# Two heads side by side in the rows of TensorE's array, in 48 rows each, for the narrow attentions' scores

## Chip, core and metric

One NeuronCore of one Trainium2 chip runs the whole program; the other cores are idle. The metric is the device time of the program in microseconds. The engines are named as in the profile: PE is TensorE's matmul, PEld its weight load, DVE VectorE, ACT ScalarE, POOL GpSimd, SP SyncE, which issues the DMAs.

## What is computed

The reference is two layers over x of shape (2, 1024, 128): a wide attention (16 heads of 64, 4 key heads, rope, low-rank additions), an expert stage with a Sinkhorn gate, a normalized narrow attention, the expert stage again, a windowed narrow attention, then a block (narrow attention and a second kind of expert stage), an RWKV scan and the same block again. The change touches the four narrow attentions, which have 16 heads of 8 channels. The block's is

```python
att = jnp.einsum('bhqd,bhkd->bhqk', q, k) / jnp.sqrt(jnp.asarray(hd, x.dtype))
att = jnp.where(causal, att, jnp.asarray(-jnp.inf, att.dtype))
att = jax.nn.softmax(att, axis=-1)
y = jnp.einsum('bhqk,bhkd->bhqd', att, v)
```

The one called "normalized" here (L0_attn_b) divides q and k by their norms first, so its scores are small and the kernel leaves out the row maximum. The windowed one (L1_attn_a) cuts queries into windows of 128 and masks each with a triangle that begins at key 0, so only the first 128 keys count.

## The kernel before

**Parts.** q and k are float32. `four_heads` splits each into three bfloat16 parts (L658 to L672 on ACT, L715 to L719 on DVE, and for the second batch entry L704 on POOL), stores them to DRAM (L511) and loads them as stacks (L491, L493): 72 partitions hold all nine products of a part of q and a part of k for the 8 channels. A score is then one bfloat16 matmul with a contraction of 72. Where the maximum is used, three further rows (72 to 74) hold the shift, split into three parts, on the q side and ones on the k side.

**Units and groups.** Four heads are a group; there are 8 groups in an attention, 4 for each batch entry. A unit is one block of 128 keys against 512 queries. A causal attention has 12 units to a group, numbered here u0 to u11: u0 to u3 (queries 0 to 511, with 512, 384, 256 and 128 of them still in play) and u4 to u11 (queries 512 to 1023, with 512 in play in u4 to u8, then 384, 256, 128). Eight of them, u0 to u3 and u8 to u11, meet the diagonal. The windowed one has 2 units to a group.

**The order on PE** is written out by hand (L629 to L644). Step u of a group does: `cols` for heads 0 and 1 (scores by key, L545; where the unit meets the diagonal and the maximum is used, a mask is added by a matmul of 128 rows, L550), some row jobs, `values` of two earlier units in every second step (L567, float32, four heads in the four 32-column tiles of the array, drained into bank 7), `cols` for heads 2 and 3, and the rest of the row jobs. ACT takes the exponentials of two heads at a time (L685); DVE and ACT move the finished sums (L656, L654), and PE turns them (L626, "divide").

**Row jobs** exist where the maximum is used: scores by query (L579) for the *next* group, one bank of PSUM each, with a mask where they meet the diagonal (L583); DVE reduces each bank to its maximum (L758). A causal group has 38: 2 "quads", 4 "pairs", 8 "three", 20 "full" (4 of them masked) and 4 "tail"; they are spread over steps 0 to 8. Steps 9 to 11 have none. They go round a ring of three banks: PE waits on `job_read` until job n-3 has been read before it writes job n (L614 to L616). After the last one DVE splits the maxima (L724 to L732), PE turns them (L621, "turn", in step 9), DVE copies them (L767), SP issues four DMAs into rows 72 to 74 of the q stack (L501), and `cols` of u0 of the next group waits for them (L539).

Of the kernel before, what the change touches and what calls it, by code (L numbers as in the profile page):

```python
# [388 lines left out]
PBUFS, LAG = 4, 2  # L389


def row_jobs(nk):
# [3 lines left out]
    return ([("quads", (a, a + 1), 0) for a in (0, 2)] + [("pairs", (i,), 1) for i in range(4)]  # L396
# [4 lines left out]
def side_jobs(ng, nu, nk, use_max, lead):  # L401
# [34 lines left out]
def four_heads(S, Q, K, V, AO, nk, tri, use_max, SLOTS):  # L436

    units, PS, nu, ng = units_of(nk), S.PS, len(units_of(nk)), B * NH // 4  # L440
# [8 lines left out]
    rows_of_stack = 75 if use_max else 72  # L449
# [3 lines left out]
    chunks = [(split_b(x)[:, b, :], dst, b) for b in range(B)  # L453
              for x, dst in ((Q, S.q_parts), (K, S.k_parts.rearrange("b d j h t -> b j d h t")))]
# [13 lines left out]
    with phase(S, 27) as (block, sems):  # L468
# [10 lines left out]
        def slot(g, i):  # L479
            return 4 * (g % SLOTS) + i  # L480

        @block.sync
        def _(sp):
            def load_group(g):
                b, h0 = divmod(4 * g, NH)
                if g >= SLOTS:
                    sp.wait_ge(cols_ready, 2 * nu * (g - SLOTS + 1))
                sp.wait_ge(stored[b], 16 * 6)
                at = slice(slot(g, 0), slot(g, 0) + 4)
                for copy in range(3):  # L490
                    sp.dma_start(S.Kst[24 * copy:24 * (copy + 1), at, :],  # L491
                                 S.k_parts[b, :, :, h0:h0 + 4, 0:keys].rearrange("d j h t -> (d j) h t")).then_inc(loaded[g % SLOTS], 16)
                    sp.dma_start(S.Qst[copy:72:3, at, :],  # L493
                                 S.q_parts[b, :, :, h0:h0 + 4, :].rearrange("j d h t -> (j d) h t")).then_inc(loaded[g % SLOTS], 16)

            def load_c(e):
# [3 lines left out]
                for i in range(4):  # L500
                    sp.dma_start(S.Qst[72:75, slot(g, i), HALF * sides[0]:HALF * (sides[-1] + 1)],  # L501
                                 S.ct[w * i:w * (i + 1), k % 2, :]).then_inc(c_loaded[g % SLOTS], 16)

            if use_max:
                for row in range(72, 75):
                    sp.dma_start(S.Kst[row:row + 1, :, :], S.ones_b[0:4 * SLOTS * keys // P, :]).then_inc(ones_set, 16)
            def store_batch(b):
                for i in range(3):
                    for n in (2 * b, 2 * b + 1):
                        sp.wait_ge(part_done, 2 * i + n % 2 + 6 * b + 1)  # L510
                        sp.dma_start(chunks[n][1][b, i].rearrange("d h t -> h d t"), S.parts[:, n % 2, i, :]).then_inc(stored[b], 16)  # L511

            store_batch(0)
            for g in range(max(lead, 1)):
                load_group(g)
            for e in turns:
# [15 lines left out]
        def _(pe):  # L532
            def cols(U, i):
# [1336 lines left out]
```

## Time and profile before

| | us |
|---|---|
| median of three runs | 2785.84 |
| lowest, highest | 2783.70, 2789.19 |
| profiled execution, own time | 2787.93 |
| its span, first to last instruction | 2786.2 |

The narrow attentions take the stretches 1150 to 1346 (normalized), 1536 to 1672 (windowed), 1701 to 2030 and 2306 to 2633 us (the two blocks') of the span. A page lists busy time by engine, then the costliest groups of instructions by source line: busy time and mean duration, and the idle time in front of them with what ended it. In a timeline each row gives start, length, engine, line, operation, shapes (partitions x elements; for a matmul contraction*columns of the array), and how many instructions of the kind follow one another; the bracket is the engine's idle time before and what ended it. PEclk and the ninth column of a stretch's row are TensorE's granted clock as a share of 2.4 GHz.

### The profile page before, as it was taken

To read this page: it belongs to the slowest core of one execution; us is meant where nothing else is said; L and a number is where in the kernel's file an instruction comes from. 1 tells how busy PE (TensorE), PEld (TensorE's weight loads), DVE (VectorE), ACT (ScalarE), POOL (GpSimd) and SP (SyncE) were. 2 spreads that over 40 slices of the span, in tenths; PEclk is the share of its full clock that TensorE was granted. 3 is DMA by queue.
4 is the path that set the end of the run, shared out by engine and by line. 5 is a ranking of instruction groups with operands and counts; after the bars stand their busy time and mean duration, and the time that the engine had idled before them with its cause. 6 is when DMAs were issued, how large, how long until landed. Compare 5 with 4: busy or idle time off the path is not lost. (4 is left out here: it accounts for less than half of the span.)

```text
span 2786.2 us, 37366 instructions
## 1 busy us (share of the span) xinstructions
PE 2224.0 (80%) x13838; PEld 1285.9 (46%) x13838; DVE 1588.6 (57%) x3402; ACT 1437.1 (52%) x2136; POOL 804.1 (29%) x384
## 2 busy tenths in 40 slices
PE   4999999999999718499619485999979425999888
PEld 2656666666666415333315243344347212444357
DVE  4777777776776445411355444777433685777324
ACT  2666676666766351388542243455642312555541
POOL 2677777776776201322001203100000022000000
PEclk8899999999999858699759696899989656999999
DMA  2000000000000130321310312211010002210000
GB/s 71 8 1 1 3 8 1 3 8 1 1 3 1 53 103 1 81 67 35 100 56 1 93 33 56 61 36 36 2 31 1 1 0 70 64 36 19 1 31 16
DMA packets 41660, 82.91 MB, mean 30 GB/s; under 512 B 10744, under 2 KB 18472, under 8 KB 37320
## 3 DMA queue, kind: packets, MB, share of 16 engines
q1 hardware_dynamic: 41480, 80.52, 10.7%
q8 instruction: 112, 1.84, 0.3%
q14 instruction: 68, 0.56, 0.1%
HBM read 66.11 MB, written 13.63 MB: 29 GB/s over the span
## 5 line engine op out<-in xcount | busy, mean ns | idle before, releaser
L685 ACT ACTIVATE probs<-psum_banks 128x1024 f32<-128x1024 f32 (+3 forms) x608 | 474.3, 826 | 367.2 <-PE psum_banks L550 260.0
L1096 POOL TENSOR_SCALAR l0a_rows<-l0a_rows,l0a_rinv 128x1024 f32<-128x1024 f32 x192 | 562.2, 2935 | 253.5 <-DVE l0a_rinv L1074 253.3
L758 DVE TENSOR_REDUCE neg_max<-psum_banks 128x1 f32<-128x512 f32 (+3 forms) x672 | 398.8, 658 | 201.4 <-PE psum_banks L583 149.7
L1062 DVE TENSOR_REDUCE l0a_nmax<-psum_banks 128x1 f32<-128x1024 f32 x256 | 312.9, 1222 | 208.7 <-PE psum_banks L955 208.0
L545 PE MATMUL psum_banks<-q_stack,k_stack 75*128 75x512 bf16 (+7 forms) x1216 | 324.9, 345 | 74.5 <-ACT probs L685 25.6
L1009 ACT ACTIVATE l0a_rows<-psum_banks,l0a_nmax 128x1024 f32<-128x1024 f32 x256 | 285.9, 1117 | 81.8 <-DVE l0a_nmax L1062 79.3
L579 PE MATMUL psum_banks<-k_stack,q_stack 72*128 72x128 bf16 (+3 forms) x1024 | 250.3, 328 | 78.1 <-DMA q_stack<-q_parts 66.5
L969 PE MATMUL psum_banks<-packed,l0a_rows 128*128 128x128 f32 x2048 | 267.7, 274 | 7.8 <-POOL l0a_rows L1096 6.3
L954 PE MATMUL psum_banks<-l0a_kh,l0a_qw 128*128 128x512 f32 x512 | 257.4, 503 | 6.1 <-DVE l0a_qw L1030 5.8
L969 PEld LDWEIGHTS psum_banks<-packed,l0a_rows 128*128 128x128 f32 x2048 | 237.9, 141 | 52.5 <-POOL l0a_rows L1096 11.5
L567 PE MATMUL psum_banks<-probs,v_ones 128*32 128x512 f32 (+3 forms) x2432 | 245.8, 520 | 7.5 <-ACT o_sum L654 6.5
L545 PEld LDWEIGHTS psum_banks<-q_stack,k_stack 75*128 75x128 bf16 (+1 forms) x1216 | 106.5, 101 | 254.6 <-ACT probs L685 104.5
L955 PE MATMUL psum_banks<-l0a_kl,l0a_qw 128*128 128x512 f32 x512 | 205.8, 402 | 0.0
L579 PEld LDWEIGHTS psum_banks<-k_stack,q_stack 72*128 72x128 bf16 x1024 | 95.3, 105 | 201.8 <-DVE neg_max L758 90.3
L954 PEld LDWEIGHTS psum_banks<-l0a_kh,l0a_qw 128*128 128x128 f32 x512 | 97.8, 191 | 134.6 <-issue 79.0
L1004 ACT ACTIVATE x_norm<-psum_banks 128x512 f32<-128x512 f32 x128 | 75.9, 593 | 136.8 <-PE psum_banks L969 136.7
L1677 POOL TENSOR_TENSOR rw_b<-rw_k,rw_o 128x1024 f32<-128x1024 f32 x2 | 4.0, 1998 | 459.2 <-DVE rw_o L1692 459.2
L550 PE MATMUL psum_banks<-tri_k,ident_b 128*128 128x128 bf16 (+1 forms) x576 | 133.8, 249 | 0.0
L1623 DVE SCALAR_TENSOR_TENSOR l1f_y<-psum_banks,rt_g,l1f_y 128x128 f32<-128x128 f32 x256 | 72.1, 344 | 103.5 <-PE psum_banks L1561 103.5
L1585 ACT ACTIVATE l1f_h<-psum_banks 128x512 f32<-128x512 f32 x128 | 75.7, 599 | 105.5 <-PE psum_banks L1547 105.2
L981 PE MATMUL psum_banks<-x_norm,l0a_v 128*64 128x512 f32 x512 | 124.0, 604 | 3.7 <-ACT l0a_ot L1014 3.7
L1547 PE MATMUL psum_banks<-x_norm_t,l1f_w 128*128 128x512 f32 x256 | 115.7, 610 | 12.4 <-DMA l1f_w<-in_l1f_w 10.8
(270 smaller groups left out, 3420.9 us busy)
## 6 DMA issues: line engine op xcount, KB each, us to landing
q_stack<-q_parts SPq DMA_DIRECT2D x96, 192.0 KB
k_stack<-k_parts SPq DMA_DIRECT2D x72, 192.0 KB
qkv<-in_l0f_w SPq DMA_DIRECT2D x6, 1024.0 KB, 5.3
q_parts<-parts SPq DMA_DIRECT2D x24, 256.0 KB
k_parts<-parts SPq DMA_DIRECT2D x24, 256.0 KB
moe_b<-in_l0f_b SPq DMA_DIRECT2D x32, 128.0 KB, 4.7
l1f_w<-in_l1f_w SPq DMA_DIRECT2D x16, 256.0 KB, 4.9
moe_w<-in_l0f_w SPq DMA_DIRECT2D x2, 1024.0 KB, 5.5
```

The costliest lines, as they stand in the source:

```text
L545: m = pe.matmul(PS[:, bank, c0:HALF], S.Kst[0:rows_of_stack, slot(g, i), kt * P:(kt + 1) * P], S.Qst[0:rows_of_stack, slot(g, i), side * H ...
L550: m = pe.matmul(PS[:, bank, c0:c1], S.ident_b[:], S.tri_k[:, 0:c1 - c0], start=False, stop=True, skip_group_check=True)
L567: m = pe.matmul(PS[32 * i:32 * (i + 1), 7, c0:HALF], S.Vx[:, NT * b + kt, h0 + i, :], S.Pt[:, U % PBUFS, i, c0:HALF], start=kt == 0, stop= ...
L579: return pe.matmul(bank[:, at:at + k1 - k0], S.Qst[0:72, slot(g, i), jq * P:(jq + 1) * P], S.Kst[0:72, slot(g, i), k0:k1], start=first, st ...
L685: act.activation(S.Pt[:, U % PBUFS, 2 * half:2 * half + 2, c0:HALF], PS[:, bank:bank + 2, c0:HALF], ACT.Exp).then_inc(exp_done, 1)
L758: dve.tensor_reduce(out, scores, AX, ALU.max, negate=True).then_inc(job_read, 1)
L954: pe.matmul(scores(s)[:, c0:c0 + HALF], q, R.Kh[:, b, c0:c0 + HALF], start=True, stop=False)
L955: m = pe.matmul(scores(s)[:, c0:c0 + HALF], q, R.Kl[:, b, c0:c0 + HALF], start=False, stop=True)
L969: m = pe.transpose(PS[:, 4 + a, jj * P:(jj + 1) * P], R.Pr[:, (NT * ps + 2 * jj + a) % RING, kt * P:(kt + 1) * P], S.ident[:])
L1009: act.activation(R.Pr[:, s % RING, :], scores(s), ACT.Exp, bias=R.nmax4[:, s % 4:s % 4 + 1], accum_out=R.rsum4[:, s % 4:s % 4 + 1]).then_i ...
L1062: dve.tensor_reduce(R.nmax4[:, s % 4:s % 4 + 1], scores(s), AX, ALU.max, negate=True).then_inc(max_done, 1)
L1096: pool.tensor_scalar(R.Pr[:, s % RING, :], R.Pr[:, s % RING, :], R.rinv4[:, s % 4:s % 4 + 1], None, ALU.mult).then_inc(pool_normed, 1)
```

## The change

The three smallest of the nine products are left out: parts (i, j) of q and k are multiplied only where i + j is at most 2, which makes six products of 8 channels, 48 rows (51 with the shift). Heads 0 and 2 of a group lie in partitions 0 to 50, heads 1 and 3 in 64 to 114. The two matmuls of a `cols` call follow one another, one in each half of the array's rows, and the two masks come behind both. Row jobs are issued two at a time, the matmuls of the two alternating, then their masks; the wait on `job_read` is that of the second of the two, taken ahead of both. The spread of jobs over steps is in twos (6 in step 0, 4 in steps 1 to 8; before 5, 4, 4, 4, 5, 4, 4, 4, 4). k's parts are stored six times instead of three (9 stores to a batch entry instead of 6), the stacks are loaded by 8 DMAs of 2/3 of the bytes instead of 6, and the ones (L506) are written by 6 DMAs behind the first loads instead of 3 ahead of the stores. Sizes of tiles in SBUF halve.

```diff
-PBUFS, LAG = 4, 2
+PBUFS, LAG, PRODUCTS = 4, 2, 6 * HD8
...
-    return ([("quads", (a, a + 1), 0) for a in (0, 2)] + [("pairs", (i,), 1) for i in range(4)]
+    return ([("quads", (a, a + 2), 0) for a in (0, 1)] + [("pairs", (i,), 1) for i in range(4)]
...
-        for k, e in enumerate(events):
-            steps[s0 + k * n // len(events)].append(e)
+        for k in range(0, len(events), 2):
+            steps[s0 + k * n // len(events)] += events[k:k + 2]
...
-    rows_of_stack = 75 if use_max else 72
+    rows_of_stack = PRODUCTS + 3 if use_max else PRODUCTS
...
+    key_blocks = ((0, 1, 2), (3, 4), (5,))
...
-            return 4 * (g % SLOTS) + i
+            return 2 * (g % SLOTS) + i // 2
+
+        def half(i, r0, r1):
+
+            return slice(64 * (i % 2) + r0, 64 * (i % 2) + r1)
...
-                sp.wait_ge(stored[b], 16 * 6)
-                at = slice(slot(g, 0), slot(g, 0) + 4)
-                for copy in range(3):
-                    sp.dma_start(S.Kst[24 * copy:24 * (copy + 1), at, :],
-                                 S.k_parts[b, :, :, h0:h0 + 4, 0:keys].rearrange("d j h t -> (d j) h t")).then_inc(loaded[g % SLOTS], 16)
-                    sp.dma_start(S.Qst[copy:72:3, at, :],
-                                 S.q_parts[b, :, :, h0:h0 + 4, :].rearrange("j d h t -> (j d) h t")).then_inc(loaded[g % SLOTS], 16)
+                sp.wait_ge(stored[b], 16 * 9)
+                at = slice(slot(g, 0), slot(g, 0) + 2)
+                for i in range(2):
+                    heads = slice(h0 + i, h0 + i + 3, 2)
+                    sp.dma_start(S.Kst[half(i, 0, PRODUCTS), at, :],
+                                 S.k_parts[b, :, :, heads, 0:keys].rearrange("c d h t -> (c d) h t")).then_inc(loaded[g % SLOTS], 16)
+                    for r0, parts in ((0, 3), (24, 2), (40, 1)):
+                        sp.dma_start(S.Qst[half(i, r0, r0 + HD8 * parts), at, :],
+                                     S.q_parts[b, 0:parts, :, heads, :].rearrange("j d h t -> (j d) h t")).then_inc(loaded[g % SLOTS], 16)
...
-            def cols(U, i):
-                (g, u), n = divmod(U, nu), (4 * U + i) // 2
+            def cols(U, h):
+                (g, u), n = divmod(U, nu), 2 * U + h
...
+                masks = use_max and meets(units[u])
+                for i in (2 * h, 2 * h + 1):
+                    rows = half(i, 0, rows_of_stack)
+                    m = pe.matmul(PS[:, 2 * (n % pairs) + i % 2, c0:HALF], S.Kst[rows, slot(g, i), kt * P:(kt + 1) * P],
+                                  S.Qst[rows, slot(g, i), side * HALF + c0:(side + 1) * HALF], start=True, stop=not masks,
+                                  skip_group_check=True)
+                c1 = HALF if tri == "window" else c0 + P
+                for i in range(2 if masks else 0):
+                    m = pe.matmul(PS[:, 2 * (n % pairs) + i, c0:c1], S.ident_b[:], S.tri_k[:, 0:c1 - c0], start=False,
                                   stop=True, skip_group_check=True)
...
+            def scores(two):
+
+                n, g = number[two[-1]], two[0][1]
+                if n >= len(ring):
+                    pe.wait_ge(job_read, n - len(ring) + 1)
...
+                for k in range(len(pieces(two[0]))):
+                    last = []
+                    for e in two:
+                        i, jq, c0, k0, k1 = pieces(e)[k]
+                        rows = half(i, 0, PRODUCTS)
+                        last.append(pe.matmul(spare(e, HALF)[:, c0:c0 + k1 - k0], S.Qst[rows, slot(g, i), jq * P:(jq + 1) * P],
+                                              S.Kst[rows, slot(g, i), k0:k1], start=k == 0, stop=False, skip_group_check=True))
+                for e, m in zip(two, last):
+                    if e[2][0] != "full" or e[2][2] == 3:
+                        m = cover(e)
+                    m.then_inc(job_ready, 1)
...
-                mid = sum(e[0] == "rows" for e in events) // 2 if U >= 0 else 0
+                mid = sum(e[0] == "rows" for e in events) // 4 * 2 if U >= 0 else 0
...
-        S.Qst, S.Kst = S.sb("q_stack", [P, 4 * SLOTS, T], BF16), S.sb("k_stack", [P, 4 * SLOTS, P * nk(NT - 1)], BF16)
+        S.Qst, S.Kst = S.sb("q_stack", [P, 2 * SLOTS, T], BF16), S.sb("k_stack", [P, 2 * SLOTS, P * nk(NT - 1)], BF16)
```

`pieces(e)` lists the matmuls of a row job as `scores` made them before, and `cover(e)` is its mask.

## Rows read from the trace of the kernel before

**Rows 1.** The page: busy time, and the costliest groups of the narrow attentions.

```profile
PE 2224.0 (80%) x13838; PEld 1285.9 (46%) x13838; DVE 1588.6 (57%) x3402; ACT 1437.1 (52%) x2136; POOL 804.1 (29%) x384
...
L758 DVE TENSOR_REDUCE neg_max<-psum_banks 128x1 f32<-128x512 f32 (+3 forms) x672 | 398.8, 658 | 201.4 <-PE psum_banks L583 149.7
...
L545 PE MATMUL psum_banks<-q_stack,k_stack 75*128 75x512 bf16 (+7 forms) x1216 | 324.9, 345 | 74.5 <-ACT probs L685 25.6
```

**Rows 2.** Stretches: one steady group of the block's attention. Columns as named.

```profile
core 0: us, PE busy (x) PEld busy (x) DVE busy (x) ACT busy (x) POOL busy (x), PEclk, DMA share, GB/s
...
1856.00:1890.00 34.00, 31.73 (x258) 14.64 (x255) 24.46 (x50) 19.98 (x27) 0.00 (x0) 1.00 0.16 36
```

**Rows 3.** Timeline of PE, same group: first matmul of u0, u5, u9, and around values.

```profile
1860.45 0.38 PE L545 MATMUL psum_banks<-q_stack,k_stack 75*128 75x512 bf16 x1 [0.93 <-issue]
...
1871.86 0.59 PE L579 MATMUL psum_banks<-k_stack,q_stack 72*128 72x512 bf16 x2
1872.29 0.59 PE L545 MATMUL psum_banks<-q_stack,k_stack 75*128 75x512 bf16 x2
...
1874.22 0.39 PE L579 MATMUL psum_banks<-k_stack,q_stack 72*128 72x512 bf16 x1 [0.15 <-DVE neg_max L758]
...
1881.19 0.66 PE L579 MATMUL psum_banks<-k_stack,q_stack 72*128 72x512 bf16 x2
1881.78 1.92 PE L567 MATMUL psum_banks<-probs,v_ones 128*32 128x512 f32 x16
1883.64 0.60 PE L545 MATMUL psum_banks<-q_stack,k_stack 75*128 75x512 bf16 x2
...
1886.73 0.33 PE L545 MATMUL psum_banks<-q_stack,k_stack 75*128 75x384 bf16 x1
```

**Rows 4.** Timeline of DVE and SP, same group.

```profile
1861.64 4.28 DVE L758 TENSOR_REDUCE neg_max<-psum_banks 128x4 f32<-128x512 f32 x7 [5.51 <-PE psum_banks L583]
...
1872.27 5.21 DVE L758 TENSOR_REDUCE neg_max<-psum_banks 128x1 f32<-128x512 f32 x9 [0.99 <-PE psum_banks L579]
...
1884.50 3.68 DVE L758 TENSOR_REDUCE neg_max<-psum_banks 128x1 f32<-128x512 f32 x6 [1.41 <-PE psum_banks L579]
...
1890.15 3.00 SPq L501 DMA_DIRECT2D q_stack<-c_turned  x4
```

**Rows 5.** Timeline of PE, wide attention: matmuls of 8 rows between ones of 128.

```profile
824.82 0.71 PE L924 MATMUL psum_banks<-l0a_ob,l0a_oa 8*128 8x128 f32 x4
825.46 0.50 PE L954 MATMUL psum_banks<-l0a_kh,l0a_qw 128*128 128x512 f32 x1
825.79 0.39 PE L955 MATMUL psum_banks<-l0a_kl,l0a_qw 128*128 128x512 f32 x1
826.02 0.40 PE L954 MATMUL psum_banks<-l0a_kh,l0a_qw 128*128 128x512 f32 x1
```

**Rows 6.** Timeline of PE, windowed attention: four row jobs between two cols calls.

```profile
1618.42 0.39 PE L579 MATMUL psum_banks<-k_stack,q_stack 72*128 72x128 bf16 x4
1618.65 0.38 PE L583 MATMUL psum_banks<-tri_q,ident_b 128*128 128x512 bf16 x1
...
1620.27 0.38 PE L545 MATMUL psum_banks<-q_stack,k_stack 75*128 75x512 bf16 x1
```

**Rows 7.** Timeline of ACT, normalized attention, from 1261.5 us; and its stretch.

```profile
1268.04 7.01 ACT L685 ACTIVATE probs<-psum_banks 128x256 f32<-128x256 f32 x8 [0.98 <-PE psum_banks L545]
1275.39 3.56 ACT L685 ACTIVATE probs<-psum_banks 128x1024 f32<-128x1024 f32 x4 [0.34 <-PE psum_banks L545]
...
1240.00:1260.00 20.00, 18.55 (x153) 6.75 (x145) 2.48 (x6) 17.14 (x24) 4.70 (x9) 1.00 0.25 60
```

**Rows 8.** Stretches: last group of the first block's attention, which has no row jobs.

```profile
1995.00:1998.00 3.00, 1.75 (x16) 0.83 (x12) 0.00 (x0) 1.25 (x2) 0.00 (x0) 1.00 0.02 3
1998.00:2001.00 3.00, 2.78 (x22) 1.20 (x23) 0.00 (x0) 2.13 (x4) 0.00 (x0) 0.53 0.00 0
...
2007.00:2010.00 3.00, 2.43 (x16) 0.67 (x8) 0.00 (x0) 1.41 (x3) 0.00 (x0) 0.76 0.00 0
```

**Rows 9.** Start of the first block's attention: last store, first load, first row job.

```profile
1708.36 0.52 SPq L511 DMA_DIRECT2D k_parts<-parts  x1
...
1711.25 0.33 SPq L491 DMA_DIRECT2D k_stack<-k_parts  x1
...
1720.51 0.61 PE L579 MATMUL psum_banks<-k_stack,q_stack 72*128 72x128 bf16 x4 [20.57 <-DMA q_stack<-q_parts]
```

More of the change, by code:

```diff
@@ L515, in _ @@
                 load_group(g)
+            for i in range(2 if use_max else 0):
+                for row in range(PRODUCTS, PRODUCTS + 3):
+                    sp.dma_start(S.Kst[half(i, row, row + 1), :, :], S.ones_b[0:2 * SLOTS * keys // P, :]).then_inc(ones_set, 16)
             for e in turns:
@@ L539, in cols @@
                     pe.wait_ge(c_loaded[g % SLOTS], c_landed(next(e for e in turns if e[1] == g and side in e[2])))
                     if U == 0:
[L541 to L542 removed]
+                        pe.wait_ge(ones_set, 96)
+                if n >= pairs:
                     pe.wait_ge(exp_done, n - pairs + 1)
[L544 to L547 removed]
@@ L611, in scores @@
-                return m
+                    return [(i, j, 0, 0, HALF)]
+                if kind == "tail":
+                    return [(i, j, 0, HALF, T)]
+                if kind == "three":
+                    return [(i, j, 0, (j - 2) * P, (j + 1) * P)]
+                if kind == "pairs":
+                    return [(i, 1, 0, 0, 2 * P), (i, 5, 2 * P, HALF, HALF + 2 * P)]
+                if kind == "quads":
+                    return [(h, 4 * a, P * (2 * n + a), HALF * a, HALF * a + P) for n, h in enumerate(heads) for a in range(2)]
@@ new lines, in pieces, with cover @@
+                return [(i, 4 * j + n, P * n, 0, P) for n in range(4)]
+            def cover(e):
+                bank, (kind, _, j) = spare(e, HALF), e[2]
+                if kind in ("tail", "three") or kind == "full" and j == 3:
+                    c0 = 2 * P if kind == "three" else 3 * P
+                    out = bank[:, c0:c0 + P].unsqueeze(1)
+                elif kind == "pairs":
+                    out = bank.rearrange("p (n c) -> p n c", n=2)[:, :, P:]
+                else:
+                    out = bank.rearrange("p (n c) -> p n c", n=4)
+                return pe.matmul(out, S.ident_b[:], S.tri_q[:].unsqueeze(1).to_broadcast([P, out.shape[1], P]), start=False,
+                                 stop=True, skip_group_check=True)
@@ L613, in side_job, with side_jobs_of @@
+            def side_jobs_of(events):
+                rows = [e for e in events if e[0] == "rows"]
+                for k in range(0, len(rows), 2):
+                    scores(rows[k:k + 2])
+                for e in events:
+                    if e[0] != "rows":
+                        side_job(e)
             def side_job(e):
```

92 lines of the change are left out of this document (23 added, 69 removed).

## Prediction

> **What bounds the kernel now.** I read the page first, then the four stretches of the narrow attentions, then one steady group instruction by instruction. The page says PE is the busiest engine and that L545, one of the two lines halved here, has 325 us [rows 1]; from that alone one would expect a large gain. The stretch of one group says less: PE 31.7, DVE 24.5 and ACT 20.0 us busy of 34.0 [rows 2]. But a matmul's length is not what it holds PE for: two of 512 columns (0.59) are followed 0.43 later by the next, so one holds PE 0.215 us, and N columns N/2400 us [rows 3]. Counted that way a group has on PE: cols 7.7 (4 heads x 4608 columns), row jobs 7.7, their masks 1.7 each, values 7.7 plus 1.5 of gaps around them, turns 0.9, together 28.9 of 34.0 us.
>
> The rest is waits. DVE reduces 38 banks a group at one per 0.60 us (5.21 for nine) [rows 4], with the two divides (0.54 each) 23.5 us, and it has to do them within steps 0 to 8. Then comes a chain that hardly uses PE: split, turn, copy, four DMA issues, landing. DVE's reduces end at 1888.2, the DMAs are issued until 1893.15, `cols` of the next u0 starts at 1894.44 (34.0 after 1860.45, the rows of SP stand 34.0 apart too), and DVE is idle 5.51 us per group for it [rows 3, 4]. So a group is 26.3 us of steps 0 to 8 (1860.45 to 1886.73) [rows 3] and 7.7 of steps 9 to 11, of which the last 4.8 are that chain. For steps 0 to 8, take for each step the longer of PE's sum and DVE's: 3.0, 2.7, 2.9, 3.1, 3.0, 2.6, 2.9, 3.7, 2.4 = 26.3. The agreement tells me that now one engine's slack in a step is made good by the ring of three banks, and that DVE sets about half of the steps. If PE cost nothing DVE would still take 23.5, so no more than 2.8 us of 34 can be had.
>
> **The change, part by part.** *Fewer rows, two heads at once.* A contraction of 51 rather than 75 saves nothing by itself. Two matmuls in the two halves of the rows: no row of this trace has such a pair. Bounds: 0.43 for two of 512 (one after the other) and 0.215 (wholly beside each other). The nearest row is values: 16 matmuls of 512 columns, four column tiles, in 1.86 including the gaps, a quarter of what they would take in turn [rows 3]. I take 0.215 + 0.03. That removes 0.185 from each full-width pair: at most 24 cols calls and 19 pairs of jobs, 7.7 - 1.3 = 6.4 us of PE per group. The Trainium skill (TensorE: Matmul & The Clock Gate, Part 3) measured four row tiles at 3.07 times the speed of one; by that share the pair would take about 0.28 instead of 0.245, an estimate that adds 0.035 x 43 = 1.5 us of PE per group; no run here shows it yet.
>
> *Changes of the array's shape.* Masks stay matmuls of 128 rows. Where now everything but values has one shape, each masked cols call becomes half rows, full rows, half rows, and so does each masked pair of jobs: 16 + 11 calls, 54 changes a group. The price of one: into values 0.16 (1881.19 + 0.43 to 1881.78) and, at the five other values of the group, 0.10; out of them 0.15 (1881.78 + 1.71 to 1883.64) [rows 3]. For tiles of rows, four matmuls of 8 rows take 0.64 where their columns need 0.43, and the first full one behind them holds PE 0.33 instead of its twin's 0.23 [rows 5]. Bounds 0 (half and full rows might not exclude each other) to 0.16; I take 0.13, nearest the values row since it is bfloat16 on one side. 54 x 0.13 = 7.0 us: more than the 6.4 saved. PE's sum per group is no smaller after the change. The Trainium skill (TensorEngine Tiling, Key Properties) says that changing the tiling mode, not just the tile, drains TensorE. It makes no exception for rows against full; it speaks against the lower bound.
>
> *Jobs in twos over a ring of three.* The second of a pair may not be written until the job three before it, the first of the pair before, has been read. So while PE makes a pair, DVE has one bank in hand, 0.60 us, where it now has two. The loop: matmul start to reduce start 0.41 (1871.86 to 1872.27), reduce 0.68, read to next matmul 0.07 (1872.27 + 2 x 0.60 + 0.68 = 1874.15 to 1874.22) [rows 3, 4]: 1.16 to 1.2 without mask, level with DVE's 1.20 a pair; with a mask 0.245 + 0.13 + 0.25 + 0.75 = 1.38 to 1.43, with quads 1.6. And slack no longer carries over, so I take the longest of PE, DVE and loop for each *half* step (a pair of jobs with the cols call, and values, behind it). Example u7: pair 0.245, values 1.71 + 0.25, cols 0.245 = 2.45, then DVE 1.20: 3.65. u1: pair 0.19 + 0.13 + 0.11 + 0.13, values 0.64 + 0.12, cols 0.19 + 0.37 = 1.87, then 1.32: 3.19. All: 4.47, 3.19, 3.11, 3.63, 2.40, 2.88, 2.94, 3.65, 2.75 = 29.0, against 26.3. PE's own sum in these steps is 22.3 and DVE's 23.9: what costs is that each waits for the other. With changes at 0 it is 27.2. Steps 9 to 11 keep their 4.8 us chain; the turn comes 0.1 to 0.2 later, as two masked calls stand before it. Per steady group +2.8; there are six and a half per block stage, +18. The first group's 14 jobs, at half clock, lose some 0.4 per pair to the loop, +3; the last group, without jobs, gains 0.18 on eight calls and loses 0.08 on sixteen: 0. Two block stages: **+42**.
>
> *Windowed attention.* PE is nearly dense. Four jobs now take 1.85 (1618.42 to 1620.27) [rows 6]. After: the second pair starts 0.3 + 0.13 + 0.42 + 0.75 = 1.6 behind the first and takes 0.3 + 0.13 + 0.44 + 0.13: 2.6. Twice a group, six groups, +9. A cols call goes from 0.88 to 0.245 + 0.26 + 0.44 = 0.95, 32 calls: +2. The first sixteen jobs: +3. Together **+14**.
>
> *Normalized attention.* No masks, no jobs; ACT is 17.1 of 20 us busy. Cols get shorter by 0.185, which only shortens ACT's two gaps of 0.34 per group; the two of 0.98 lie behind values and stay, and one has a divide in front that now costs two changes more (+0.2) [rows 7]. -0.4 x 8, and -1 for the start at half clock: **-4**.
>
> *DMA.* Nine stores instead of six (some 0.75 MB more before the first load), ones moved out of the way (-0.8 of issue), loads of 768 instead of 1152 KB into the first group (now 9.3 from 1711.25 to 1720.51, with stores ending 2.4 after their last issue) [rows 9]. -3 for the load, +2 to +3 for the stores: 0, bounds -3 to +3 in each of four stages. Later loads are under cover of a group each. The new wait (16 * 9) holds ACT for the second batch's parts only as long as the stores take; behind it are exponentials. The split parts' arithmetic does not change.
>
> **Sum.** 42 + 14 - 4 + 0 = +52 on the profiled execution's 2787.9, which lies 2 above the median: 2838 against a median of 2786, 1.9% slower.
>
> **The rivals.** *Clock falls.* In the last group, with no row jobs, PE was 1.75 of 3 us busy at full clock and then the granted clock was 0.53, 0.5 until it rose in the stretch from 2007, so near 10 us at 1.2 GHz [rows 8]; the second block's last group looks alike. In steady groups before, it held at 1.00 [rows 2]. After, PE streams columns for about 20 of 37 us instead of 27 of 34. If the clock falls once a group, some 10 us at half rate add to u0 to u3, where the PE-bound halves grow by about 4 us: 13 groups, +52, and up to +20 in the normalized one: 2890 to 2910. For it: rows 8. Against it: I cannot tell whether two halves at once count as more activity. The skill's clock page (TensorE: Matmul & The Clock Gate, Part 1) has the clock fall after idleness; here it fell with PE over half busy.
> *Faster: no drain, ring deep enough.* If a change of shape between half and full rows costs 0, and slack still carries over a step, the step maxima give 24.7 instead of 26.3: -1.6 - 0.3 for 13 groups = -25, the windowed stage -8 (cols 0.64 instead of 0.88), the normalized -8: 2745 to 2765. It decides below some 0.05 per change. Halfway, at 0 but with the pair's loop, the time is within 5 of now.
> *Pairs don't overlap.* Then every call also loses 0.185 and PE leads everywhere: above 2900.
>
> **How the numbers follow.** Forecast as worked out (2810 to 2865): 0.44. Clock: 0.24. No overlap: 0.05. Faster: 0.20. Within 0.2%, about what a measurement of this kernel can tell from none: 0.07. The range leaves out the upper part of the second and third and the lower part of the fourth: 2762 to 2905. Faster 0.20, same 0.07, slower 0.73.
>
> **What would show it.** Right: a steady group of 36 to 38 us; PE gaps of 0.10 to 0.15 at L545 to L550 and back; DVE's reduces in twos with 0.15 to 0.25 idle between masked pairs. Wrong: matmuls of 51 rows followed by a mask after N/2400 with no gap; a group under 34 us; PE rows of half height that start 0.2 apart; granted clock under 1.00 in steady groups.

## The result, and the profile after

The changed kernel takes 2852.56 us (median, 2845.5 to 2860.1), the kernel before 2787.52 beside it: 1.0236 times as long, 95% interval 1.0202 to 1.0269. The forecast was 2838. The time came near it and on the forecast side, but not for the reasons forecast: every stage term was mis-sized (two stages cost more than forecast, two less), and the largest part of the loss was one of the rivals, the clock.

The profiled execution has a span of 2843.8 us against 2786.2; it is the fastest of the four of the kernel after, so traces differ by 57.6 us where medians differ by 65.0. A stage is counted from the first split on ACT (L669 before, L689 after) to the end of its last exponential or eviction:

| stage | before | after | difference | forecast |
|---|---|---|---|---|
| normalized attention | 193.2 | 180.1 | -13.1 | -4 |
| windowed attention | 134.5 | 135.7 | +1.2 | +14 |
| first block's attention | 326.2 | 358.8 | +32.6 | +21 |
| second block's attention | 325.7 | 357.8 | +32.1 | +21 |
| all between and behind | 1806.6 | 1811.4 | +4.8 | 0 |

Of the last row 4.2 us lie between the two blocks, from the end of the first one's attention to the first split of the second. No kernel here changes anything in that stretch, and it took between 278.2 and 285.8 us in the twelve traces (278.5 before, 282.7 after), so I don't count it for the change.

From the page of the kernel after (it answers [rows 1]): the line of `cols`, one of the two that were halved, did shrink (L556 has 211 us, L545 had 325), but DVE's reduces (L778) now wait 256 us instead of 201, longest for the masks of the row jobs (L608).

```profile
PE 2193.6 (77%) x13828; PEld 1188.5 (42%) x13838; DVE 1604.8 (56%) x3402; ACT 1435.6 (50%) x2136; POOL 803.3 (28%) x384
...
L778 DVE TENSOR_REDUCE neg_max<-psum_banks 128x1 f32<-128x512 f32 (+3 forms) x672 | 412.6, 660 | 256.3 <-PE psum_banks L608 185.7
...
L556 PE MATMUL psum_banks<-q_stack,k_stack 51*128 51x512 bf16 (+7 forms) x1216 | 211.0, 358 | 84.6 <-ACT probs L705 39.7
```

Two steady groups of the kernel after, each from one issue of the c DMAs (L509) to the next. The columns are those of [rows 2]; PEclk is the granted clock.

```profile
1900.37:1940.40 40.03, 34.54 (x257) 11.47 (x255) 25.38 (x49) 19.99 (x27) 0.00 (x0) 0.83 0.11 21
2542.17:2577.72 35.55, 29.31 (x257) 10.46 (x255) 25.36 (x49) 19.89 (x27) 0.00 (x0) 1.00 0.11 24
```

The same instructions take 35.55 us at 1.00 and 40.03 at 0.83. Of the ten groups that the kernel before ran in 34.0 us each at 1.00, the kernel after has one at 1.00; the others read 0.83 to 0.95, and the mean of the ten is 38.4. So a group has two losses: 1.55 us at full clock, and 2.9 us because TensorE drops to the lower of its two levels (1.2 GHz) inside the group, once or twice. Where it drops, in three-us stretches of the group that begins at 1862.47:

```profile
1865.00:1868.00 3.00, 2.20 (x26) 0.79 (x18) 0.00 (x0) 0.96 (x2) 0.00 (x0) 1.00 0.36 89
1868.00:1871.00 3.00, 2.29 (x19) 0.76 (x18) 2.78 (x5) 1.47 (x2) 0.00 (x0) 1.00 0.85 157
1871.00:1874.00 3.00, 2.81 (x27) 1.05 (x26) 2.11 (x4) 1.13 (x2) 0.00 (x0) 0.65 0.11 20
...
1883.00:1886.00 3.00, 1.82 (x18) 0.70 (x20) 3.00 (x7) 2.07 (x3) 0.00 (x0) 0.93 0.00 0
1886.00:1889.00 3.00, 2.99 (x24) 0.72 (x16) 1.44 (x3) 2.03 (x3) 0.00 (x0) 0.50 0.00 0
```

The first drop follows the thin stretch around the chain (split, turn, copy, DMAs), the second the steps in which PE waits for DVE (1.82 of 3 us busy). Not every group has both: of the ten, five drop 9 to 10 us behind the issue of the c DMAs (and all five again later), four only at 20 us or later, and one not at all, though all run the same instructions. What decides between them no run shows. While the clock is low PE is busy throughout (2.99 of 3.00), since the same columns take twice as long.

Now the timeline of PE in the group that ran at full clock, to read the prices of the prediction:

```profile
2546.42 0.39 PE L556 MATMUL psum_banks<-q_stack,k_stack 51*128 51x512 bf16 x2 [0.80 <-issue]
2546.74 0.29 PE L561 MATMUL psum_banks<-tri_k,ident_b 128*128 128x128 bf16 x2
2546.96 0.40 PE L624 MATMUL psum_banks<-k_stack,q_stack 48*128 48x128 bf16 x8
...
2548.47 0.39 PE L624 MATMUL psum_banks<-k_stack,q_stack 48*128 48x256 bf16 x4
2548.79 0.39 PE L608 MATMUL psum_banks<-tri_q,ident_b 128*128 128x256 bf16 x2
2549.86 0.39 PE L624 MATMUL psum_banks<-k_stack,q_stack 48*128 48x256 bf16 x4 [0.68 <-DVE neg_max L778]
...
2560.96 0.39 PE L624 MATMUL psum_banks<-k_stack,q_stack 48*128 48x512 bf16 x2 [0.56 <-DVE neg_max L778]
2561.19 0.38 PE L556 MATMUL psum_banks<-q_stack,k_stack 51*128 51x512 bf16 x2
2562.15 0.39 PE L624 MATMUL psum_banks<-k_stack,q_stack 48*128 48x512 bf16 x2 [0.59 <-DVE neg_max L778]
...
2574.41 0.34 PE L556 MATMUL psum_banks<-q_stack,k_stack 51*128 51x384 bf16 x2
```

- Two heads side by side: 2560.96 to 2561.19, 0.23 us for two matmuls of 512 columns, where the kernel before needed 0.43 [rows 3].
- Half rows to full rows: 2546.42 to 2546.74 is 0.32, of which the pair is 0.21 (its columns) to 0.23 (as measured above): 0.09 to 0.11. Back: 2546.74 to 2546.96 is 0.22, of which two masks of 128 columns are 0.107: 0.11.
- The loop of pairs: 2560.96 to 2562.15, 1.19 without mask; 2548.47 to 2549.86, 1.39 with one; 2546.96 to 2548.47, 1.51 for quads. In each PE idles until DVE has read a bank.
- u0 to u9, 2546.42 to 2574.41: 28.0 us, against 26.3 in [rows 3].

### The profile page after: what moved, and what is told of

Read it like the earlier page. It is cut to its first block and busy times, and to the rows that moved or that the text cites. A ratio compares the mean times of both kernels' runs of the same rounds, so it can differ in the third digit from the quotient of the medians.

```text
span 2843.8 us, 37453 instructions
## 1 busy us (share of the span) xinstructions
PE 2193.6 (77%) x13828; PEld 1188.5 (42%) x13838; DVE 1604.8 (56%) x3402; ACT 1435.6 (50%) x2136; POOL 803.3 (28%) x384
## 5 line engine op out<-in xcount | busy, mean ns | idle before, releaser
L778 DVE TENSOR_REDUCE neg_max<-psum_banks 128x1 f32<-128x512 f32 (+3 forms) x672 | 412.6, 660 | 256.3 <-PE psum_banks L608 185.7
L577 PE MATMUL psum_banks<-probs,v_ones 128*32 128x512 f32 (+3 forms) x2432 | 272.1, 568 | 7.6 <-ACT o_sum L674 6.5
L556 PE MATMUL psum_banks<-q_stack,k_stack 51*128 51x512 bf16 (+7 forms) x1216 | 211.0, 358 | 84.6 <-ACT probs L705 39.7
L624 PE MATMUL psum_banks<-k_stack,q_stack 48*128 48x128 bf16 (+3 forms) x1024 | 150.8, 352 | 155.9 <-DVE neg_max L778 92.1
L556 PEld LDWEIGHTS psum_banks<-q_stack,k_stack 51*128 51x128 bf16 (+1 forms) x1216 | 56.8, 95 | 260.8 <-ACT probs L705 119.7
L624 PEld LDWEIGHTS psum_banks<-k_stack,q_stack 48*128 48x128 bf16 x1024 | 41.9, 99 | 257.3 <-DVE neg_max L778 185.5
L1001 PE MATMUL psum_banks<-l0a_cols,l0a_v 128*64 128x512 f32 x512 | 124.1, 605 | 0.0
```

Source lines behind the costliest of these rows:

```text
L556: m = pe.matmul(PS[:, 2 * (n % pairs) + i % 2, c0:HALF], S.Kst[rows, slot(g, i), kt * P:(kt + 1) * P], S.Qst[rows, slot(g, i), side * HALF ...
L577: m = pe.matmul(PS[32 * i:32 * (i + 1), 7, c0:HALF], S.Vx[:, NT * b + kt, h0 + i, :], S.Pt[:, U % PBUFS, i, c0:HALF], start=kt == 0, stop= ...
L624: last.append(pe.matmul(spare(e, HALF)[:, c0:c0 + k1 - k0], S.Qst[rows, slot(g, i), jq * P:(jq + 1) * P], S.Kst[rows, slot(g, i), k0:k1], ...
L778: dve.tensor_reduce(out, scores, AX, ALU.max, negate=True).then_inc(job_read, 1)
L1001: m = pe.matmul(PS[HD * a:HD * (a + 1), 6, :], R.V[:, v // STEPS % B, kt, :], (R.Pc, R.Pd)[v // 2 % 2][:, v % 2, a, :], start=kt == 0, sto ...
```

## The experiments

Theory A: the loop of pairs and the changes of shape make the block stages slower. The rival: the clock makes them slower, because PE now streams less. The other numbers below are of steady groups, ten in each run (the mean of the kernel after is 38.4 us; two of the expectations quoted below have it as 38.6):

| kernel | ratio to before | group at clock 1.00 | mean of ten | granted clock in them |
|---|---|---|---|---|
| before | 1 | 34.0 | 34.0 | 1.00 |
| after | 1.0236 | 35.55 | 38.4 | 0.83 to 1.00 |
| masks in half rows | 1.0163 (1.0133 to 1.0193) | 34.5 | 36.4 | 0.79 to 1.00 |
| single waits | 1.0356 (1.031 to 1.0402) | none | 43.0 | 0.73 to 0.95 |
| both | 1.0024 (1.0011 to 1.0037) | 33.9 | 34.8 | 0.91 to 1.00 |
| extra matmuls, one stretch | 1.0291 (1.0266 to 1.0316) | 36.9 | 39.2 | 0.84 to 1.00 |
| single waits, extra matmuls in one stretch | one run, 2873.82 | 37.2 | 40.4 | 0.80 to 1.00 |
| extra matmuls, both stretches | 1.0157 (1.0136 to 1.0178) | 37.3 | 37.3 | 1.00 |
| before without masks | one run, 2818.65 | 33.1 | 36.4 | 0.82 to 1.00 |
| all heads in one half | one run, 3102.35 | none | 51.8 | 0.65 to 0.70 |
| both, all heads in one half | one run, 3120.49 | none | 46.35 | 0.70 to 0.84 |
| normalized attention alone | 0.9938 (0.9917 to 0.9959) | 34.0 | 34.0 | 1.00 |

**Masks in half rows** (e1_halfmasks). A second copy of identity and masks has its row halves swapped, so that each head's mask is made in its own half:

```diff
-                for i in range(2 if masks else 0):
-                    m = pe.matmul(PS[:, 2 * (n % pairs) + i, c0:c1], S.ident_b[:], S.tri_k[:, 0:c1 - c0], start=False,
-                                  stop=True, skip_group_check=True)
+                for part in range(2 if masks else 0):
+                    for i in range(2):
+                        rows = half(i, 0, 64)
+                        m = pe.matmul(PS[:, 2 * (n % pairs) + i, c0:c1], (S.ident_b, S.ident_s)[part][rows, :],
+                                      (S.tri_k, S.tri_ks)[part][rows, 0:c1 - c0], start=False,
+                                      stop=part == 1, skip_group_check=True)
```

> The changed kernel, but the causal and window masks are no longer matmuls of 128 rows: each is two matmuls of 64 rows, in the half of the array's rows in which its head's scores were made (with a second copy of the identity and of the masks whose row halves are swapped), and the masks of two heads lie side by side as the scores do. So the columns cost the same and the 54 changes between half and full rows of a steady group are gone. Theory A (shape changes, 0.11 us each, and the loop of job pairs over three banks made the block stages slower): a steady group falls by 2 to 3 us (step sum 27.2 instead of 29.0, and the masked loop falls from 1.4 to 1.2 us a pair), the block stages by 26 to 38 us together, the windowed stage by 3 to 6: ratio to the kernel before 1.007 to 1.013, from 1.024. Theory B (the lower clock inside steady groups is the whole of it, and the gaps at the changes lie in idle time): no shorter than by 8 us, ratio 1.020 to 1.024, or longer if fewer full-row matmuls let the clock fall more. Theory C (changes cost only where PE leads; the pair coupling is all): ratio 1.018 to 1.022, groups keep 38 us.

Measured 1.0163, between A and B and outside the range of each theory. At full clock a group fell from 35.55 to 34.5 us, so the 54 changes cost 1.0 us of a group, much less than the 5 to 6 us that they hold PE for; PE also waits for DVE in these steps, and I take it that most changes lie in that time. The mean of the ten fell by 2.0 us, so about half of that gain is clock. The two block stages became 24.5 us shorter together. But 6 us went into making the copies at the start (this kernel's first split comes at 1157.3, not 1150.7), and the windowed stage took 142.3 instead of 135.7, as its first groups ran at 0.50 and 0.62 where the kernel after had 0.57 and 1.00. The clock still fell in eight of the ten block groups.

**Single waits** (e2_single), masks of full rows as in the changed kernel:

```diff
-                n, g = number[two[-1]], two[0][1]
+                g = two[0][1]
+                if len(two) == 2 and len(pieces(two[0])) == 1:
+                    scores(two[:1])
+                    scores(two[1:])
+                    return
+                n = number[two[-1]]
```

> The changed kernel, with masks of full rows, but the row jobs made of one piece (32 of 38 a group) wait each for its own bank, one after the other, as in the kernel before; only quads, pairs and the windowed jobs of several pieces stay in twos. A masked pair now changes the shape four times instead of twice, 16 changes more a group, 1.8 us of PE. Theory A: the coupling was worth about 1.5 to 2 us a group and the changes take 1 of it back: steady groups 0.5 to 1 us shorter, ratio to before 1.018 to 1.022. Theory B (coupling costs nothing, shape changes all): steady groups 1 to 2 us longer, ratio 1.028 to 1.035. Theory C (coupling is all): groups fall to 35, ratio 1.005 to 1.010.

Measured 1.0356, worse than any theory said. Eight of ten groups took 44.4 us at a granted clock of 0.73; the two at 0.95 took 37.1 and 37.6, which is what the changed kernel's own group at 0.95 takes (37.2). So it is the clock that makes this kernel slow, and of theory A's gain of 0.5 to 1 us nothing can be seen at equal clock. Why the clock falls harder here stays open. Jobs issued one by one seldom lie side by side, and the runs with all heads in one half below had low clocks; but the next kernel issues its jobs one by one too, and of all kernels with the changed row jobs and no extra matmuls its clock fell least.

**Both edits** (e3_both):

> Both edits at once: masks in half rows and one-piece row jobs with a wait each. No shape change is left but around values, turns and divides, and slack carries over from step to step. Theory A: the sum over the steps comes to 25 to 26.5 us as in the rival 'no drain, ring deep enough', a steady group to 33 to 34.5 us, the whole to 0.990 to 1.002 of the kernel before (the normalized stage gives 13 us of that). Theory B (the granted clock falls inside groups whatever else is done, since PE streams fewer columns): groups stay at 36 or more, ratio 1.010 to 1.020. If the two edits are not additive, this run against the two others says so.

Measured 1.0024 with the 6 us of copies in it, and 326.3 and 327.7 us in the block stages, as before the change (326.2 and 325.7). Its groups at full clock:

```profile
1849.15:1883.02 33.87, 28.92 (x311) 12.51 (x309) 24.55 (x49) 19.68 (x27) 0.00 (x0) 1.00 0.12 25
```

33.9 against 34.5 with the pair's wait: the coupling costs 0.6 us a group. PE is 2.8 us less busy than before the change [rows 2], and the group is only 0.1 shorter: that fits the prediction's first part, by which DVE (24.5) and the chain set it. With neither changes nor coupling the block stages are back where they were, not below. The clock still fell in six of the ten groups, for 0.9 us a group in the mean, and not always behind the thinnest stretch: in the group from 1883.02 PE was busy for 1.57 and 1.79 of 3 us in the stretches from 1886 and 1889 and kept 1.00, and the clock fell at about 1908, behind stretches with 2.6 to 2.9 us busy.

**Extra matmuls in one thin stretch** (e5_filler), and the same on the kernel with single waits (e6_single_filler):

```diff
+                for _ in range(0 if not use_max or nu < 4 or U == 0 else 4 if u == 0 and h == 0 else 1 if u >= 9 else 0):
+                    pe.matmul(PS[:, 2 * (n % pairs), :], S.ident_b[:], S.tri_k[:], start=True, stop=True, skip_group_check=True)
                 if h == 0 and use_max and kt == 0:
                     pe.wait_ge(c_loaded[g % SLOTS], ...
```

The wait on `exp_done` is moved ahead of the extra matmuls, since they write the bank that it guards.

> The changed kernel with PE kept busy in the thin stretch at the end of each group of the two block stages: one extra matmul of 128 rows and 512 bfloat16 columns (0.213 us at full clock) before each cols call of u9 to u11, and four before the first cols call of a group, while it waits for the DMAs of the c rows; they write the bank that the real matmul then overwrites. Ten a group, 2.1 us of PE, of which 0.85 lie in a wait; the others may lengthen u9 to u11 by 0.2 each at most, 1.2 us. Theory K (the clock: the granted clock falls some 9 us into a group because PE does little in and just before the chain; the changed kernel's group is 35.5 us at clock 1.00 and 37 to 40 us otherwise, 38.6 in the mean): the granted clock stays at 1.00 in most steady groups, they take 35.5 to 36.5 us, and the whole comes to 1.008 to 1.014 of the kernel before, from 1.024. Rival (the fall has nothing to do with PE's activity ahead of it, or comes from the pairs themselves): clock 0.83 to 0.95 as now and groups of 39 to 40 us, ratio 1.025 to 1.030.

Measured 1.0291: the rival's number, but not its reason. Only three of the ten groups still have a drop near 10 us; nine have a drop somewhere, mostly from 22 us on. In the group of this kernel that begins at 1872.22 the first drop is gone and the second is there:

```profile
1881.00:1884.00 3.00, 2.81 (x36) 1.23 (x32) 2.63 (x5) 1.22 (x2) 0.00 (x0) 1.00 0.35 54
1884.00:1887.00 3.00, 2.54 (x21) 0.98 (x20) 2.31 (x4) 2.08 (x4) 0.00 (x0) 1.00 0.02 5
...
1890.00:1893.00 3.00, 1.92 (x20) 0.44 (x12) 1.94 (x5) 1.88 (x3) 0.00 (x0) 1.00 0.00 0
1893.00:1896.00 3.00, 2.33 (x26) 0.89 (x28) 2.83 (x6) 1.58 (x2) 0.00 (x0) 0.85 0.00 0
1896.00:1899.00 3.00, 2.78 (x14) 0.45 (x12) 1.63 (x4) 2.71 (x4) 0.00 (x0) 0.50 0.00 0
```

> The kernel with single waits and masks of full rows (whose steady groups locked at 44.4 us with the granted clock at 0.73), with the same ten extra matmuls a group. Theory K: without the fall a group takes 36 to 37.5 us (the one group whose clock was 0.95 took 37.1), so the time falls by 60 to 80 us, to 2810 to 2830. Rival (the extra shape changes of the single jobs make the 44 us themselves): groups stay over 43 us, time 2885 or more.

Measured 2873.8 in one run; the forecast of 2810 to 2830 was missed. But the groups no longer stay at 44.4: one took 37.2 (clock 1.00), two 38.5 (0.96), five 40.7 (0.87), two 43.3 (0.80). There too the extra matmuls moved the drop rather than ended it: where eight of ten groups had dropped twice, near 9 and near 26 us, five now drop once, near 23 us.

**Extra matmuls in both thin stretches** (e9_filler2), with a pair of half rows before each cols call of u3 to u6 besides:

```diff
+                for i in range(2 if use_max and nu >= 4 and U and 3 <= u <= 6 else 0):
+                    pe.matmul(PS[:, 2 * (n % pairs) + i, :], S.ident_b[half(i, 0, 64), :], S.tri_k[half(i, 0, 64), :], start=True, stop=True,
+                              skip_group_check=True)
```

> The changed kernel with the ten extra matmuls of the filler run (whose stretch from 9 us on then kept the full clock, while the clock fell from about 23 us on, behind the thin stretch of u4 to u6) and with more in that second thin stretch: before each cols call of u3 to u6 one pair of extra matmuls of 64 rows and 512 columns, side by side in the two halves, into the banks that the call then overwrites; 0.22 us a pair, eight pairs a group, 1.8 us of PE in steps in which PE waits for DVE. Theory K (each fall follows a thin stretch of PE): both falls go, the granted clock is 1.00 in nearly all steady groups, they take 36.9 to 37.8 us, as much as or less than the changed kernel's mean of 38.6 though PE does 4 us more; the two block stages sum to 700 to 712 us, ratio to before 1.015 to 1.022. Rival (the falls come whatever is added, or from half rows as such): clock 0.83 to 0.95, groups over 39 us, ratio 1.03 or more.

Measured 1.0157. All ten steady groups are alike, and the two block stages sum to 701.8 us instead of 716.6:

```profile
1858.76:1896.06 37.30, 32.81 (x281) 11.68 (x281) 25.34 (x49) 20.14 (x27) 0.00 (x0) 1.00 0.11 23
```

This shows what the clock costs, and that PE's own work brings it back. The kernel does all that the changed one does and about 4 us of useless columns in each group, and by the two ratios it is 0.8% faster; its steady groups differ from the changed kernel's in the extra matmuls and in the clock, which no longer falls. A group is 1.75 us longer than the changed kernel's at full clock and 1.1 us shorter than its mean.

**Less work before the change** (e8_before_nomask). The kernel before, its mask matmuls left out (so hidden keys are attended to):

```diff
-                              stop=not (use_max and meets(units[u])), skip_group_check=True)
-                if use_max and meets(units[u]):
-                    c1 = HALF if tri == "window" else c0 + P
-                    m = pe.matmul(PS[:, bank, c0:c1], S.ident_b[:], S.tri_k[:, 0:c1 - c0], start=False,
-                                  stop=True, skip_group_check=True)
+                              stop=True, skip_group_check=True)
...
-                    m = hide(bank.rearrange("p (n c) -> p n c", n=4))
```

> The kernel before, with the mask matmuls of the windowed attention and of both block stages left out (the output then attends to hidden keys); nothing else differs. PE streams some 3.4 us less of columns in a steady group of 34. It has no half rows and no shape change but those of values. Theory K (the clock follows what PE streams, not the half rows): the granted clock falls under 1.00 in some steady groups, which then take 34 to 37 us, though there is less work; groups at 1.00 take 32.5 to 33.5 us. Rival (only half-row pairs or shape changes bring the fall): clock 1.00 throughout, groups of 32.5 to 33.5 us, 2765 to 2775 in all.

Measured 2818.65 in one run, 33.6 us more than the kernel before on the same chip, with no half rows and 3.4 us less to do in a group. The two block stages are 20 us longer in its trace than in that of the kernel before, and the clock fell in eight of the ten steady groups. Two neighbours of its groups:

```profile
1791.48:1824.59 33.11, 29.10 (x201) 10.87 (x201) 24.35 (x49) 19.48 (x27) 0.00 (x0) 1.00 0.16 37
...
1824.59:1862.00 37.41, 34.41 (x201) 12.87 (x201) 24.78 (x49) 19.69 (x27) 0.00 (x0) 0.82 0.14 33
```

So no pair of half rows is needed for the fall, and no change of shape but those around `values`. The kernel before kept its full clock with little to spare: taking 3.4 us of columns from a group was enough to lose it in most groups.

**All heads in one half** (e7_onehalf; e10_both_onehalf is the same edit on the kernel with both edits):

```diff
-            return 2 * (g % SLOTS) + i // 2
+            return 4 * (g % SLOTS) + i
...
-            return slice(64 * (i % 2) + r0, 64 * (i % 2) + r1)
+            return slice(r0, r1)
```

> The changed kernel with all four heads in the lower half of the array's rows (slots for four heads as in the kernel before), so nothing lies side by side: same instructions, same waits, same changes between half and full rows, but each pair of 512 columns must hold PE 0.43 us instead of 0.21 to 0.23. It prices the overlap. If the overlap is what the trace reads (0.2 us for each of 43 full-width pairs): PE gets 6 to 8 us more a group, a steady group takes 39 to 42 us at full clock, the windowed stage 10 us more and the normalized one goes back to 190 or more: 2890 to 2930 us. And it shows what the clock follows: PE streams as many columns as in the kernel before, though over fewer rows; if time spent streaming counts, the granted clock stays at 1.00 in steady groups, if rows or shape changes count, it falls as in the changed kernel.

> Masks in half rows and single waits, with all four heads in the lower half of the rows: no change between half and full rows is left but around values, turns and divides, and nothing lies side by side. Against the run with both edits, which differs only in the half of every second head, it prices the overlap without shape changes, and against the run with one half and masks of full rows it takes the shape changes away. If what made the granted clock fall there to 0.70 were the shape changes, it is 0.95 to 1.00 here, with groups of 37 to 40 us. If it is that PE streams over half the rows at a time only, the clock falls again to 0.7 to 0.8 in steady groups, which take 43 to 49 us. Overlap by the windowed stage at full clock: its groups take 13.2 to 14.5 us instead of 11.85.

Measured 3102.35 and 3120.49, one run each. The first is far over its forecast of 2890 to 2930; the second had no forecast for the whole, its steady groups average 46.35 us (42.9 to 51.0) where 43 to 49 was expected if the clock fell, and its windowed groups did not run at full clock. What the overlap is worth can be read where the clock is 1.00 in both e7_onehalf and the kernel after: windowed groups of 13.7 us against 12.0. The normalized stage, most of it at full clock in both, took 197.6 against 180.1. Most of the rest is clock. First a windowed and a block group of e7_onehalf, then of e10_both_onehalf:

```profile
1641.47:1655.20 13.73, 11.46 (x81) 4.52 (x81) 7.31 (x18) 4.98 (x7) 0.00 (x0) 1.00 0.13 35
1952.71:2003.69 50.98, 48.96 (x257) 15.03 (x257) 25.57 (x49) 20.45 (x27) 0.00 (x0) 0.70 0.10 17
```

```profile
1646.88:1675.54 28.66, 27.13 (x99) 10.37 (x98) 7.30 (x18) 5.08 (x7) 0.00 (x0) 0.50 0.06 17
1984.51:2035.52 51.01, 49.24 (x313) 23.19 (x311) 25.77 (x49) 20.47 (x27) 0.00 (x0) 0.70 0.10 17
```

The windowed groups of e10_both_onehalf run at 0.50 from end to end, with PE busy 27.1 of 28.7 us and no wait of note, where the kernel with both edits, which differs only in that heads, and the two parts of their masks, lie side by side, took 11.85 us at 1.00. In the block groups, taking the shape changes away (and the wait of pairs with them) helped but did not bring the clock back: 0.70 to 0.84 and 46.35 us in the mean against 0.65 to 0.70 and 51.8. So with nothing side by side the clock was lower in every pair of runs that can be compared: 0.65 to 0.70 against the changed kernel's 0.83 to 1.00, 0.70 to 0.84 against 0.91 to 1.00 with both edits, and 0.50 against 1.00 in the windowed groups, though PE was busy for a larger share of the time. The prediction could not tell whether two halves at once count as more activity; by these rows, two heads side by side held the clock better than the same heads one after another. How rows and time are weighed, no run here tells.

**The change for the normalized attention alone** (e4_mixed): in the two block stages and the windowed one the functions of the kernel before are called.

```diff
+        S.k_parts3 = nc.dram_tensor("k_parts3", (B, HD8, 3, NH, T), BF16).ap()
...
-    turn = narrow_attention(S, *S.qkv, lambda j: 1, "window", True)
+    turn = narrow_attention_3(S, *S.qkv, lambda j: 1, "window", True)
...
-        turn = narrow_attention(S, *S.qkv, lambda j: j + 1, "diag", True)
+        turn = narrow_attention_3(S, *S.qkv, lambda j: j + 1, "diag", True)
```

> The six products in half rows for the normalized attention only; the windowed attention and the two block stages run the code of the kernel before, nine stores and three layouts of it included. If the stages are independent, as the two traces read (normalized stage 180.1 instead of 193.2 us from the first split to the last exponential), the whole is 13 us under the kernel before: ratio 0.994 to 0.997, about 2774 us. Rival: the normalized stage was faster by chance of that execution's clock or loads, or its gain is given back by the stage behind it: 0.998 to 1.001.

(In those stages the stores are six to a batch entry, as in the kernel before, and not nine.)

Measured 2772.72 us, ratio 0.9938 (0.9917 to 0.9959): faster than both kernels. Its normalized stage took 180.1 us, its windowed one 134.7, its steady block groups 34.0 at 1.00. The block stages as a whole read 323.4 and 322.0, 3 to 4 us less than in the trace of before with the same code. The difference lies in the end of each, from the last steady group's end on: 66.8 and 65.2 us at a granted clock of 0.97 and 1.00, where the kernel before took 69.5 and 69.4 at 0.93. Why the clock fell less there no run shows, and the stretches outside the attentions were 7.0 us longer in this trace, so that its span is 12.4 us shorter than before while the medians differ by 16.3.

## Why the prediction was right, and where it was not

*What bounds the kernel.* Right. With PE relieved of changes and coupling a group stays at 33.9 us. DVE's floor was taken too high: the text charges 0.60 us for each of 38 reduces (and gives the sum once as 23.5 and once as 23.9), but the eight of 384 columns start 0.47 apart (1866.79, 1867.25 in the trace of before), which makes some 22.7 with the divides.

*Fewer rows, two heads at once.* 0.215 + 0.03 taken, 0.23 measured. The Trainium skill (TensorE: Matmul & The Clock Gate, Part 3) has a speedup of 3.07 for four row tiles, from which the prediction's estimate was 0.28. For two halves of 64 rows the trace decides, 0.23.

*Changes of shape.* 0.13 taken, about 0.1 measured. The Trainium skill (TensorEngine Tiling (Array Packing), Key Properties) says that changing the tiling mode drains TensorE. The gaps of 0.09 to 0.11 us between half and full rows agree with that. The step sums gave them 1.8 us of a group (29.0 less 27.2); taken away they gave 1.0.

*Jobs in twos.* The loops came as worked out: 1.19, 1.39, 1.51 for 1.16 to 1.2, 1.38 to 1.43 and 1.6. The step that failed is the rule of summing the longest of each half step: it gave 29.0 us for u0 to u8, and 28.0 was measured. So slack still carries over in part. So the steady group's own term was +1.55, not +2.8, and the coupling's share of it 0.6.

*The clock.* The forecast left it at 1.00 and gave the fall a chance of 0.24, at one drop a group and +4 us. It happened in nine of ten steady groups, for 2.9 us a group in the mean, and told in the group before them, where the clock came up later (38.1 us at 0.64 against 33.0 at 0.83). For the first block: 1.5 us up to the first c DMAs, 1.4 and 5.1 in the next two groups, 23.8 in the five steady ones (7.8 of them at full clock and 16.0 by the clock), 0.7 at the end, 32.6 in all with the decimals. For this the forecast of +42 for two block stages was 23 short. The rival's +52 for the clock in thirteen groups was too high in turn: 29 in the ten steady ones, and no more than 10.6, all that they grew by, in the two ahead of them.

*Windowed attention.* +14 forecast, +1.2 measured. PE in one group of the kernel after:

```profile
1604.04 0.40 PE L624 MATMUL psum_banks<-k_stack,q_stack 48*128 48x128 bf16 x8
1604.37 0.60 PE L608 MATMUL psum_banks<-tri_q,ident_b 128*128 128x512 bf16 x2
1605.55 0.40 PE L624 MATMUL psum_banks<-k_stack,q_stack 48*128 48x128 bf16 x8 [0.57 <-DVE neg_max L778]
...
1606.41 0.39 PE L556 MATMUL psum_banks<-q_stack,k_stack 51*128 51x512 bf16 x2
```

Four jobs take 2.37 us, where 2.6 was forecast and 1.85 is in [rows 6], and a group 12.0 instead of 11.3: +0.7 where the terms gave some +1.8. The start, forecast at +3, shrank by 1.3 up to the c DMAs issued at 1606.26 before and 1591.11 after: its first two stretches grew by 2.5 us together at a lower clock (0.52 and 0.57 for 0.67 and 0.65), but in the third the clock was already at 1.00 where it had read 0.79, 9.0 us for 12.8.

*Normalized attention.* -4 forecast, -13.1 measured. ACT, one group of the kernel after:

```profile
1254.01 4.88 ACT L705 ACTIVATE probs<-psum_banks 128x256 f32<-128x256 f32 x8 [0.88 <-PE psum_banks L556]
1259.86 12.36 ACT L705 ACTIVATE probs<-psum_banks 128x256 f32<-128x256 f32 x16 [0.97 <-PE psum_banks L556]
```

Before, the same exponentials stood in four runs with gaps of 0.34, 0.34, 0.98 and 0.98 [rows 7]: 17.72 us of runs and 2.64 of gaps. Now they stand in two: 17.24 and 1.85. The two short gaps went, and with each of them the head of a run: an exponential that finds its bank ready starts before the one ahead has ended (in the trace of before, at 1275.39 and 1276.31: 0.92 apart, 1.02 long). The prediction counted 0.4 a group for the gaps and nothing for the runs; it was 1.3, eight times, and about 3 us at the start.

*Sum.* +52 forecast, +57.6 measured. The agreement is partly luck: -9 in the normalized and -13 in the windowed stage against +23 in the blocks and +5 outside. Of the prediction's own signs of being wrong one came, a granted clock under 1.00 in steady groups, and a steady group took 35.55 us at full clock and 38.4 in the mean, neither within its 36 to 38. What was only argued: that the later rise of the clock in the first groups is the same effect. No run isolated it.

## What to carry to other kernels

Before taking work from an engine that is not the bound, look at the granted clock of the stretches that it makes thinner: here 3.4 us less of columns in a group of 34 made it 0.9 us shorter while the clock held, and 2.4 us longer in the mean of ten. Where one engine waits for another in turn, price an edit from the loop (start, read, next start), and let slack carry over unless a wait forbids it. And ask of each stage by itself: the same edit gave 13 us in the stage that ACT sets and lost 32 in each stage that DVE and PE share.

## What the hardware showed that was not expected

- A change between half and full rows costs PE about 0.1 us each way (0.09 to 0.11); two matmuls of 512 columns in the two halves hold it for 0.22 to 0.23 us.
- The granted clock stayed at 0.50 with PE busy 27.1 of 28.7 us, on half rows one after another, where side by side it was 1.00 with PE busy 9.35 of 11.85. The Trainium skill (TensorE: Matmul & The Clock Gate, Part 1) says that the clock is set by how busy PE has been recently. By busy time alone the first of these stretches should have had the higher clock, so here the measurement decides.
- A kernel can be slower with less work and faster with useless work: 2818.65 us without masks (one run) against 2785.05 with them, and 1.0157 with 4 us of extra matmuls a group against 1.0236 without.
